# A two-layer graph network: moving the graph product off fp32 and staggering three groups over an unrolled slot schedule

## The chip, the core and the metric

The kernel runs on one core of a Trainium2 chip. A core has five engines that run their own instruction queues in order and meet only through semaphores: TensorE (PE, with its weight loads shown as PEld), VectorE (DVE), ScalarE (ACT), GpSimd (POOL) and SyncE (SP), which here issues every DMA. The metric is the device time of one execution in microseconds (us), lower is better.

## What is computed

`x` has 128 graphs of 128 nodes with 256 features, `adj` is one dense 128 by 128 matrix of weights. Layer 0 is a graph product, a 256 by 256 product, a residual and a layer norm. Layer 1 is three steps of a gated update in which `in_mat` and `out_mat` are both `adj`, then a residual and a layer norm.

```python
x = layernorm(x + (adj @ x) @ W0 + b0)
h = x
for _ in range(3):
    a = adj @ h;  av = concat(a, a)
    z = sigmoid(av @ w3.T + b3 + h @ u3.T + bu3)
    r = sigmoid(av @ w4.T + b4 + h @ u3.T + bu3)
    hv = tanh(av @ w5.T + b5 + (r * h) @ u5.T + bu5)
    h = (1 - z) * h + z * hv
out = layernorm(x + h)
```

Since both halves of `av` are equal, both kernels add the two halves of w3, w4 and w5 once. They also put w3 - w4 in the place of w3, so that z's sum is r's sum, already in PSUM, plus one more product.

## The kernel before

**Tiles.** The 128 graphs go in 32 groups of `G` = 4. A state is kept with features on the partitions: `[128, C=2, 512]`, 512 columns being 4 graphs of 128 nodes. Each gate product is split in three single-pass products, high by high, low by high and high by low (`split_product`, L307): 12 matmuls of 128x512. The high part is a ScalarE copy to fp32r (`copy`, L463), the low part a VectorE subtraction (`low_part`, L577). A gated slot has five of them (u3, w4, w5, w3, u5), 60 matmuls.

**Graph product.** `graph` (L317) is done in plain fp32: the state with nodes on the partitions (`h_nat`) is the stationary operand, `adjt` the moving one, in 8 matmuls of 128x128 columns, each recorded as two. Its result in PSUM (`ps_x`) has features on the partitions already, so that ScalarE and VectorE read its high and low parts (`a_hi`, `a_lo`) straight from PSUM, with no DMA between.

**State to nodes.** For the next graph product the new state must be turned: VectorE transposes blocks of 32x32 (`state_blocks`, L687), SyncE writes them to DRAM (`to_dram`, L214) and reads them back with the four blocks of partitions exchanged (`to_quadrants`, four DMAs, L220), and ScalarE copies them into `h_nat`. The same trip brings a normed first state (`first_blocks`, L629) and a last state (`last_state_blocks`, L638) to the other layout.

**Stages.** Groups go in 16 pairs. A pair has six slots (`SLOTS`): steps 0 to 2 of group a and of group b, in turn. Within slot i the other group's graph product stands between the two output halves of u5. Layer 0 of the next pair is spread over the slots of this one: its graph product (`first_graph`) in slots 1 and 3, its weight product (`first_weights`, L350, 24 matmuls of 128x256) in slots 2 and 4, its sum, statistics and norm on VectorE. GpSimd adds `b0` to x in `x_bias` (L847). `run_pairs` unrolls the first and the last pair and runs the 14 between as a loop on every engine. The state update on VectorE is three operations on each half of 512 columns: L674 (hv - h), L678 (times z), L680 (plus h).

## Time and profile before

| | us |
|---|---|
| median of 3 runs (lowest, highest) | 1674.75 (1674.03, 1675.79) |
| the profiled execution | 1671.51 |
| its span in the trace | 1669.7 |
| TensorE, matmuls at work | 1643.2 |
| VectorE at work | 1364.2 |
| ScalarE at work | 836.8 |
| GpSimd at work | 162.4 |
| moved by DMA in the span | 166.48 MB |

The span is the time from the first to the last record of the profiled execution. Busy times are sums of the durations that the profiler recorded; a matmul's recorded end is modelled and overlaps the next one's start, so the distance between starts is what a matmul costs. An engine's idle time counts only if something on the way to the end waits for it. TensorE's granted clock is full (1.00) over the stretch shown with the rows.

### The profile page before, as it was taken

How to read it: one execution, taken by the hardware profiler on the slowest of the kernel's cores; microseconds unless marked ns; L12 is line 12 of the kernel's file. 1: busy time of each engine (PE TensorE's matmuls, PEld its weight loads, DVE VectorE, ACT ScalarE, POOL GpSimd, SP SyncE). 2: the span in 40 equal slices, each digit the busy share in tenths (PEclk: the TensorE clock that was granted, in tenths of full speed). 3: DMA queues.
4: the chain of work that ended last, by engine and by line, in shares of the span. 5: the costliest groups of instructions: out<-in, count | busy, mean ns of one | idle time of the engine just before them, and what ended most of it. 6: DMA issues, size and time to landing. Idle time of an engine off the chain costs nothing.

```text
span 1669.7 us, 24669 instructions
## 1 busy us (share of the span) xinstructions
PE 1643.2 (98%) x8608; PEld 1410.7 (84%) x8608; DVE 1364.2 (82%) x2217; ACT 836.8 (50%) x1190; POOL 162.4 (10%) x168
## 2 busy tenths in 40 slices
PE   6999999999999999999999999999999999999997
PEld 6888888888888888888888888888888888888885
DVE  5678888888888888888888878888888888888777
ACT  3445454554545454545445454545455455545553
POOL 3001001010100101001010010100101010010000
PEclk8999999999999999999999999999999999999998
DMA  3123242232422333224232332424224232243221
GB/s 112 51 76 126 82 125 83 88 126 96 123 87 83 126 109 105 88 88 136 90 118 83 99 115 88 126 82 125 84 86 126 98 125 86 82 128 110 91 75 63
DMA packets 172021, 166.48 MB, mean 100 GB/s; under 512 B 16352, under 2 KB 147936, under 8 KB 172000
## 3 DMA queue, kind: packets, MB, share of 16 engines
q1 hardware_dynamic: 172000, 166.20, 31.2%
q8 instruction: 13, 0.21, 0.1%
q14 instruction: 8, 0.07, 0.0%
HBM read 84.35 MB, written 81.79 MB: 100 GB/s over the span
## 4 chain that ended last, share of the span: by engine, by line
PE 91%; DVE 4%; SPq 1%; DMA 1%; issue 1%; ACT 1%; DVEq 0%
PE ps_r L307 44%; PE ps_h L307 29%; PE ps_x L317 10%; PE ps_z L350 5%; PE ps_z L317 3%; DVE hv L678 1%; SPq L220 1%; DVE hv L674 1%; DMA h_moved_in<-h_scratch 1%; DVE h_blocks L687 1%; DMA x_in_b<-x 0%; DVE h_t_a L680 0%; ACT hv L499 0%; DVE w_lo L577 0%; ACT h_nat L463 0%
## 5 line engine op out<-in xcount | busy, mean ns | idle before, releaser
L558 ACT ACTIVATE z_sb<-ps_r,bias_z 128x512 f32<-128x512 f32 x192 | 129.9, 686 | 96.9 <-PE ps_r L307 96.7
L499 ACT ACTIVATE hv<-ps_h,bias_h 128x512 f32<-128x512 f32 x192 | 132.3, 689 | 86.2 <-PE ps_h L307 85.9
L674 DVE TENSOR_TENSOR hv<-hv,h_t_a 128x512 f32<-128x512 f32 x96 | 78.3, 815 | 118.9 <-ACT hv L499 118.9
L535 ACT ACTIVATE rh<-ps_r,bias_r 128x512 f32<-128x512 f32 x192 | 126.6, 684 | 91.9 <-PE ps_r L307 90.9
L678 DVE TENSOR_TENSOR hv<-hv,z_sb 128x512 f32<-128x512 f32 x192 | 160.7, 837 | 7.8
L577 DVE TENSOR_TENSOR rh_lo<-rh,rh_hi 128x512 fp32r<-128x512 f32 x192 | 128.4, 689 | 9.4
L463 ACT ACTIVATE rh_hi<-rh 128x512 fp32r<-128x512 f32 x192 | 119.6, 630 | 28.5 <-DVE rh L762 28.5
L317 PEld LDWEIGHTS ps_x<-adjt,h_nat 128*128 128x128 f32 x1024 | 123.4, 191 | 8.7 <-ACT h_nat L463 4.3
L307 PE MATMUL ps_h<-rh_hi,u_hi 128*128 128x512 f32 x384 | 127.1, 412 | 0.0
L317 PE MATMUL ps_x<-adjt,h_nat 128*128 128x128 f32 x1024 | 125.3, 275 | 1.2 <-ACT h_nat L463 1.2
L307 PE MATMUL ps_r<-a_hi_b,w_hi 128*128 128x512 f32 x384 | 121.3, 397 | 0.0
L463 ACT ACTIVATE h_hi_a<-h_t_a 128x1024 fp32r<-128x1024 f32 x48 | 50.7, 1056 | 138.2 <-DVE h_t_a L680 138.1
L307 PE MATMUL ps_r<-a_hi_a,w_hi 128*128 128x512 f32 x384 | 119.3, 392 | 0.0
L307 PE MATMUL ps_r<-a_hi_a,w_lo 128*128 128x512 f32 x384 | 118.9, 391 | 0.0
L307 PE MATMUL ps_h<-rh_hi,u_lo 128*128 128x512 f32 x384 | 118.7, 390 | 0.0
L307 PE MATMUL ps_r<-a_hi_b,w_lo 128*128 128x512 f32 x384 | 118.4, 389 | 0.0
L307 PE MATMUL ps_r<-a_lo_a,w_hi 128*128 128x512 f32 x384 | 118.4, 389 | 0.0
L307 PE MATMUL ps_r<-a_lo_b,w_hi 128*128 128x512 f32 x384 | 118.2, 389 | 0.0
L307 PE MATMUL ps_h<-rh_lo,u_hi 128*128 128x512 f32 x384 | 118.2, 389 | 0.0
L463 ACT ACTIVATE h_hi_b<-h_t_b 128x1024 fp32r<-128x1024 f32 x48 | 50.7, 1056 | 109.1 <-DVE h_t_b L680 109.1
L762 DVE TENSOR_TENSOR rh<-rh,h_t_a 128x512 f32<-128x512 f32 x96 | 64.9, 691 | 46.1 <-ACT rh L535 45.7
L674 DVE TENSOR_TENSOR hv<-hv,h_t_b 128x512 f32<-128x512 f32 x96 | 64.9, 676 | 45.0 <-ACT hv L499 44.5
(141 smaller groups left out, 3749.2 us busy)
## 6 DMA issues: line engine op xcount, KB each, us to landing
h_scratch<-h_blocks SPq DMA_DIRECT2D x128, 256.0 KB, 2.0
h_moved_in<-h_scratch SPq DMA_DIRECT2D x512, 64.0 KB, 2.0
h_scratch<-h_blocks SPq DMA_DIRECT2D x30, 512.0 KB, 2.6
x_in_a<-x SPq DMA_DIRECT2D x16, 512.0 KB, 4.7
x_in_b<-x SPq DMA_DIRECT2D x16, 512.0 KB, 5.7
out<-result_a SPq DMA_DIRECT2D x16, 512.0 KB, 3.0
h_moved_in_a<-h_scratch SPq DMA_DIRECT2D x60, 128.0 KB, 3.5
h_moved_in_b<-h_scratch SPq DMA_DIRECT2D x60, 128.0 KB, 3.0
```

The lines of the kernel that those rows point to most:

```text
L220: sp.dma_start(moved_in[to * Q:(to + 1) * Q].rearrange("q i m e -> q i (m e)"), by_target[to]).then_inc(moved, 16)
L307: mm = pe.matmul(psum[:, o, :], w[:, c, o * P:(o + 1) * P], v[:, c, :], start=start and n == 0 and c == 0, stop=stop and ends, skip_group_ ...
L317: mm = pe.matmul(psum[:, c, b * N:(b + 1) * N], nat[:, b, c * P:(c + 1) * P], adjt[:, :], start=True, stop=True)
L350: mm = pe.matmul(by_node(psum)[:, b, :], v[:, c, cols], w[:, c, :], start=n == 0 and c == 0, stop=n == 2 and c == C - 1, skip_group_check= ...
L463: return act.activation(dst, src, ACT.Copy)
L499: act.activation(hv[:, c, :], ps_h[:, c, :], ACT.Tanh, bias=bias_h[:, c:c + 1]).then_inc(hv_ready, 1)
L535: r = act.activation(rh[:, c, :], ps_r[:, c, :], ACT.Sigmoid, bias=bias_r[:, c:c + 1])
L558: z = act.activation(z_sb[:, c, :], ps_r[:, c, :], ACT.Sigmoid, bias=bias_z[:, c:c + 1])
L577: return dve.tensor_tensor(dst, full, hi.bitcast(F32), ALU.subtract)
L674: dve.tensor_tensor(hv[:, c, :], hv[:, c, :], before[:, c, :], ALU.subtract).then_inc(diff_ready, 1)
L678: dve.tensor_tensor(hv[:, c, :], hv[:, c, :], z_sb[:, c, :], ALU.mult).then_inc(scaled_ready, 1)
L762: dve.tensor_tensor(rh[:, c, :], rh[:, c, :], before[:, c, :], ALU.mult).then_inc(rh_ready, 1)
```

## The change

Everything is rewritten, in one step:

- **The graph product** is split as the gate products are: `adj` is the stationary operand in a high and a low part, the state with nodes on the partitions (`nat_hi`, `nat_lo`) the moving one: 6 matmuls of 128x512. Its result `ps_a` now has nodes on the partitions. It is turned like a state: VectorE transposes it out of PSUM (`graph_blocks`), SyncE writes it to DRAM (`write_a`) and reads it back (`read_a`) into `a_landed`, and `a_hi`, `a_lo` are made from that.
- **Slots.** Step t of group g stands in slot s = 3g + 4t. So three groups are under way, each at another step, and between two steps of one group stand three slots of other work. The slots run from -6 (layer 0 of group 0) to 101. Slots 1, 2, 5, 96, 99 and 100 have no gated step; 96 have one. Within iteration s: the graph product of slot s+1, then the u3 product of slot s, layer 0 of a later group, then the other gates of slot s.
- **Layer 0** is at s mod 3 = 0 (graph product) and 2 (weight product); a group's first state is moved at 1; the last residual and its statistics are at 1. The two norms move from VectorE to ScalarE, with a scale and a shift that GpSimd works out.
- **No loop:** all slots are written out on each engine.
- On VectorE an iteration begins with the state update of slot s-1 (three operations of 1024), then the transposes of the graph result of slot s+1.

```diff
-            def graph(psum, nat, signal):
-
-                for c in range(C):
-                    for b in range(G):
-                        mm = pe.matmul(psum[:, c, b * N:(b + 1) * N], nat[:, b, c * P:(c + 1) * P], adjt[:, :],
-                                       start=True, stop=True)
-                mm.then_inc(signal, 1)
...
+    def slot_of(g, t):
+        return 3 * g + 4 * t
...
+            def graph(s):
+                n = nth[s]
+                pe.wait_ge(nat_hi_ready, n + 1)
+                if n >= 1:
+                    pe.wait_ge(a_blocks_ready, n)
+                for c in range(C):
+                    for k, (w, v) in enumerate(((adj_hi, nat_hi), (adj_lo, nat_hi), (adj_hi, nat_lo))):
+                        if c == 0 and k == 2:
+                            pe.wait_ge(nat_lo_ready, n + 1)
+                        mm = pe.matmul(ps_a[:, c, :], w[:, :], v[:, c, :], start=k == 0, stop=k == 2,
+                                       skip_group_check=True)
+                mm.then_inc(a_done, 1)
...
+            def write_a(s):
+                n, half = nth[s], nth[s] % 2
+                sp.wait_ge(a_blocks_ready, n + 1)
+                if n >= 2:
+                    sp.wait_ge(a_moved[half], (n // 2) * MOVED)
+                to_dram(a_scratch[half], a_blocks[half][:, :, :, :].rearrange("p j c x -> p j (c x)"), a_written[half])
+
+            def read_a(s):
+                n, half = nth[s], nth[s] % 2
+                sp.wait_ge(a_written[half], (n // 2 + 1) * 16)
+                if n >= 2:
+                    sp.wait_ge(a_lo_ready, n - 1)
+                to_quadrants(a_landed[half][:, :, :, :], a_scratch[half], a_moved[half])
...
+            for s in range(BEGIN, END + 5):
+                h0_next = group_at(s, NORM + 1)
+                if h0_next is not None:
+                    write_h0(h0_next)
+                if s + 1 in nth:
+                    write_a(s + 1)
+                if h0_next is not None:
+                    read_h0(h0_next)
+                if s + 1 in nth:
+                    read_a(s + 1)
+                if (g := group_at(s, RESULT + 1)) is not None:
+                    store(g)
+                if (g := group_at(s, GRAPH - 2)) is not None and g >= 2:
+                    load(g)
+                if s - 1 in nth:
+                    move_h(s - 1)
...
+            def first_graph(g):
+                pe.wait_ge(x_loaded[g % 2], (g // 2 + 1) * 16)
+                if g >= 1:
+                    pe.wait_ge(y_added, g)
...
+            def graph_blocks(s):
+                n, half = nth[s], nth[s] % 2
+                dve.wait_ge(a_done, n + 1)
+                if n >= 2:
+                    dve.wait_ge(a_written[half], (n // 2) * 16)
+                for c in range(C):
+                    tr = dve.transpose(a_blocks[half][:, :, c, :].rearrange("p i (b e) -> p i b e", e=Q),
+                                       ps_a[:, c, :].rearrange("p (i b f) -> p i b f", b=G, f=Q))
+                tr.then_inc(a_blocks_ready, 1)
...
+            def graph_low(s):
+                n, half = nth[s], nth[s] % 2
+                dve.wait_ge(a_hi_ready, n + 1)
+                low_part(in_quadrants(a_lo[half]), chunks_first(a_landed[half]),
+                         in_quadrants(a_hi[half])).then_inc(a_lo_ready, 1)
...
+            def update(s):
+                n, (g, t) = nth[s], at(s)
+                state = chunks_first(h_t[g % H_RING])
+                dve.wait_ge(hv_ready, 2 * n + 2)
+                dve.tensor_tensor(in_quadrants(hv), in_quadrants(hv), state, ALU.subtract).then_inc(diff_ready, 1)
+                dve.wait_ge(z_ready, 2 * n + 2)
+                dve.wait_ge(diff_ready, n + 1)
+                dve.tensor_tensor(hv[:, :, :], hv[:, :, :], z_sb[:, :, :], ALU.mult).then_inc(scaled_ready, 1)
+                dve.wait_ge(scaled_ready, n + 1)
+                dve.tensor_tensor(state, in_quadrants(hv), state, ALU.add).then_inc(h_ready, 1)
...
+                if s - 1 in nth:
+                    update(s - 1)
+                if s + 1 in nth:
+                    graph_blocks(s + 1)
+                if s - 1 in nth:
+                    state_blocks(s - 1)
+                if s + 2 in nth:
+                    node_low(s + 2)
+                if s in nth:
+                    reset(s)
+                if s + 1 in nth:
+                    state_low(s + 1)
+                    graph_low(s + 1)
+                if (g := group_at(s, GRAPH)) is not None:
+                    first_graph_low(g)
+                if (g := group_at(s, WEIGHTS)) is not None:
+                    first_sum(g)
+                if (g := group_at(s, NORM)) is not None:
+                    first_blocks(g)
+                if (g := group_at(s, SUM_UP)) is not None:
+                    residual(g)
+
...
+            def add_bias(g):
+                pool.wait_ge(ax_done, g + 1)
```

**VectorE, the middle of the program.** Before, from the second half of one slot's work to the next slot (L674, L678, L680 are the update; L577 of `a_lo` reads `ps_x`; `h0_nat` is layer 0's result):

```order
L680 TENSOR_TENSOR h_t_b<-hv,h_t_b 128x512
L577 TENSOR_TENSOR a_lo_a<-ps_x,a_hi_a 128x1024
L687 STREAM_TRANSPOSE h_blocks<-h_t_b 128x4x4x32
L674 TENSOR_TENSOR hv<-hv,h_t_b 128x512
L678 TENSOR_TENSOR hv<-hv,z_sb 128x512
L680 TENSOR_TENSOR h_t_b<-hv,h_t_b 128x512
L687 STREAM_TRANSPOSE h_blocks<-h_t_b 128x4x4x32
L612 TENSOR_TENSOR h0_nat_b<-ps_z,x_bias_b 128x1024
L762 TENSOR_TENSOR rh<-rh,h_t_a 128x512 x2
L577 TENSOR_TENSOR rh_lo<-rh,rh_hi 128x512 x2
L577 TENSOR_TENSOR h_lo_b<-h_t_b,h_hi_b 128x1024
L587 BN_STATS h0_sums<-h0_nat_b 128x6 x4
```

After, one whole iteration with s mod 3 = 2 without its last row (L584, L587, L589 are the update, L549 the graph result's transposes, L501 with `a_lo` the low part that needs the trip through DRAM, L522 and L506 layer 0):

```order
L584 TENSOR_TENSOR hv<-hv,h_t_d 128x1024
L587 TENSOR_TENSOR hv<-hv,z_sb 128x1024
L589 TENSOR_TENSOR h_t_d<-hv,h_t_d 128x2x4x128
L549 STREAM_TRANSPOSE a_blocks_b<-ps_a 128x4x128 x2
L596 STREAM_TRANSPOSE h_blocks_b<-h_t_d 128x1024
L501 TENSOR_TENSOR nat_lo<-h_landed_a,nat_hi 128x1024
L574 TENSOR_TENSOR rh<-rh,h_t_c 128x512 x2
L501 TENSOR_TENSOR rh_lo<-rh,rh_hi 128x512 x2
L501 TENSOR_TENSOR h_lo<-h_t_a,h_hi 128x1024
L501 TENSOR_TENSOR a_lo_b<-a_landed_b,a_hi_b 128x1024
L522 TENSOR_TENSOR x_in_b<-ps_l,x_in_b 128x1024
L506 BN_STATS h0_sums<-x_in_b 128x6 x4
```

The low part of the graph result stood behind a ScalarE copy from PSUM; now it stands in the same iteration as the transposes, with a write to DRAM, a read and a copy between them, and layer 0's sum and the next update stand behind it in VectorE's queue.

**SyncE, the DMA queue, the middle of the program.** Before, one slot's move of the state (two halves) and the write of a first state:

```order
L220 DMA h_moved_in<-h_scratch_0 32x4x128 x4
L220 DMA h_moved_in<-h_scratch_1 32x4x128 x4
L214 DMA h_scratch_0<-h_blocks 128x512
L214 DMA h_scratch_1<-h_blocks 128x512
L220 DMA h_moved_in<-h_scratch_0 32x4x128 x4
L220 DMA h_moved_in<-h_scratch_1 32x4x128 x4
L214 DMA h0_scratch<-h0_blocks 128x1024
```

After, an iteration with s mod 3 = 1 (`a_` is the graph result, `h_t` from `h0_scratch` the first state):

```order
L188 DMA h0_scratch<-h0_blocks 128x1024
L188 DMA a_scratch_b<-a_blocks_b 128x1024
L193 DMA h_t_d<-h0_scratch 32x4x256 x4
L193 DMA a_landed_b<-a_scratch_b 32x4x256 x4
L239 DMA x_in_b<-x 128x4x256
L188 DMA h_scratch_b<-h_blocks_b 128x1024
L193 DMA h_landed_b<-h_scratch_b 32x4x256 x4
```

Each iteration now has two trips, graph result and state, in place of one, and in every third iteration the first state's write and read stand ahead of the read of the graph result.

**TensorE, the end of one slot and the start of the next.** Before:

```order
L307 MATMUL ps_h<-rh_hi,u5_lo 128x512 x2
L307 MATMUL ps_h<-rh_lo,u5_hi 128x512 x2
L317 MATMUL ps_x<-adjt,h_nat 128x128 x8
L307 MATMUL ps_h<-rh_hi,u5_hi 128x512 x2
L307 MATMUL ps_h<-rh_hi,u5_lo 128x512 x2
L307 MATMUL ps_h<-rh_lo,u5_hi 128x512 x2
L307 MATMUL ps_r<-h_hi_a,u3_hi 128x512 x2
L307 MATMUL ps_r<-h_hi_a,u3_lo 128x512 x2
```

After:

```order
L274 MATMUL ps_h<-rh_lo,u5_hi 128x512 x2
L310 MATMUL ps_a<-nat_hi,adj_hi 128x512
L310 MATMUL ps_a<-nat_hi,adj_lo 128x512
L310 MATMUL ps_a<-nat_lo,adj_hi 128x512
L310 MATMUL ps_a<-nat_hi,adj_hi 128x512
L310 MATMUL ps_a<-nat_hi,adj_lo 128x512
L310 MATMUL ps_a<-nat_lo,adj_hi 128x512
L274 MATMUL ps_r<-h_hi,u3_hi 128x512 x2
L274 MATMUL ps_r<-h_hi,u3_lo 128x512 x2
```

The graph product stands between two slots now, in 6 matmuls of 512 columns in place of 8 of 128 that are recorded twice.

## Rows read from the trace of the kernel before

**Rows 1.** engines of the whole span, page part 1: busy us (share) xinstructions.
```profile
PE 1643.2 (98%) x8608; PEld 1410.7 (84%) x8608; DVE 1364.2 (82%) x2217; ACT 836.8 (50%) x1190; POOL 162.4 (10%) x168
```

**Rows 2.** TensorE: stretch of 50 to 1650 us, and its one wait there.
```profile
50.00:1650.00 1600.00, 1598.77 (x8384) 1372.20 (x8383) 1322.27 (x2136) 814.84 (x1163) 145.26 (x148) 1.00 0.31 100
...
PE ps_x L317 <- ACT h_nat L463: 1.2, 5, 0.3
```

**Rows 3.** timeline of TensorE: start us, us, engine line operation out<-in xcount.
```profile
802.61 1.95 PE L317 MATMUL ps_z<-adjt,x_in_b 128*128 128x128 f32 x16
804.31 0.71 PE L307 MATMUL ps_r<-a_hi_b,w_hi 128*128 128x512 f32 x2
804.86 0.62 PE L307 MATMUL ps_r<-a_hi_b,w_lo 128*128 128x512 f32 x2
...
813.47 0.61 PE L307 MATMUL ps_h<-rh_lo,u_hi 128*128 128x512 f32 x2
...
819.81 0.28 PE L350 MATMUL ps_z<-w_hi,ax_hi 128*128 128x256 f32 x1
...
822.68 0.63 PE L307 MATMUL ps_r<-a_hi_a,w_hi 128*128 128x512 f32 x2
```

**Rows 4.** timeline of VectorE, half a state update (columns as in Rows 3).
```profile
1639.75 0.69 DVE L674 TENSOR_TENSOR hv<-hv,h_t_a 128x512 f32<-128x512 f32 x1 [3.13 <-ACT hv L499]
1640.48 0.69 DVE L678 TENSOR_TENSOR hv<-hv,z_sb 128x512 f32<-128x512 f32 x1
```

**Rows 5.** groups on VectorE by form: shapes xcount; busy us, mean ns; idle before.
```profile
L577 DVE TENSOR_TENSOR h_lo_b<-h_t_b,h_hi_b 128x1024 fp32r<-128x1024 f32 x48 | 58.6, 1221 | 5.5 <-ACT h_hi_b L463 5.5
...
L687 DVE STREAM_TRANSPOSE h_blocks<-h_t_b 128x512 f32<-128x512 f32 x64 | 45.2, 706 | 3.4
...
L587 DVE BATCH_NORM_STATS2 h_sums<-h_nat_a 128x6 f32<-128x256 f32 x64 | 22.4, 412 | 0.0
...
L612 DVE TENSOR_TENSOR h_nat_b<-ps_z,x_bias_b 128x1024 f32<-128x1024 f32 x15 | 18.3, 1218 | 1.2 <-PE ps_z L350 1.2
...
L594 DVE BATCH_NORM_AGGREGATE h_meanvar<-h_sums 128x2 f32<-128x6 f32 x132 | 12.3, 155 | 0.1
```

**Rows 6.** timeline of the DMA issues on SyncE (SPq), one stretch.
```profile
847.29 0.34 SPq L214 DMA_DIRECT2D h_scratch<-h_blocks  x1
849.91 1.73 SPq L220 DMA_DIRECT2D h_moved_in_b<-h_scratch  x4
851.68 0.43 SPq L214 DMA_DIRECT2D last_scratch_a<-last_blocks_a  x1
855.35 1.73 SPq L220 DMA_DIRECT2D last_moved_in_a<-last_scratch_a  x4
...
865.22 1.76 SPq L220 DMA_DIRECT2D last_moved_in_b<-last_scratch_b  x4
```

**Rows 7.** DMA from 865 to 870 us, slices of 0.125 us: busy tenths.
```profile
DMA  0000000004039557988986999987753000000000
```

**Rows 8.** one group on ScalarE by form (columns as in Rows 5).
```profile
L463 ACT ACTIVATE h_hi_b<-h_t_b 128x1024 fp32r<-128x1024 f32 x48 | 50.7, 1056 | 109.1 <-DVE h_t_b L680 109.1
```

**Rows 9.** timeline of GpSimd and VectorE, the same stretch.
```profile
862.41 2.37 POOL L847 TENSOR_TENSOR x_bias_a<-x_in_a,bias_row 128x1024 f32<-128x1024 f32 x1 [25.40 <-DMA x_in_a<-x]
864.74 2.85 POOL L847 TENSOR_TENSOR x_bias_b<-x_in_b,bias_row 128x1024 f32<-128x1024 f32 x1
...
863.95 1.38 DVE L674 TENSOR_TENSOR hv<-hv,h_t_a 128x512 f32<-128x512 f32 x1 [2.60 <-ACT hv L499]
865.45 2.68 DVE L678 TENSOR_TENSOR hv<-hv,z_sb 128x512 f32<-128x512 f32 x1
```

**Rows 10.** timeline of the whole core at its start and its end.
```profile
17.64 1.86 DVE L709 TENSOR_TENSOR w_raw<-w_raw 128x512 f32<-128x512 f32 x3
...
35.59 1.20 PE L307 MATMUL ps_r<-a_hi_a,w_hi 128*128 128x512 f32 x2
...
1665.65 1.28 SPq L291 DMA_DIRECT2D out<-result_b  x2
```

## What the change does to the time

> **What bounds the kernel now.** I read the page's engine totals first. TensorE is at work for 98% of the span, VectorE for 82%, ScalarE 50% [rows 1]. Recorded matmuls overlap, so 98% alone proves little. The next view does: from 50 to 1650 us TensorE works 1598.77 of 1600 us at full granted clock, and its only wait there is for `h_nat`, 1.2 us in five times [rows 2]. So TensorE's own stream sets the time, and a matmul costs the distance between starts. From 804.86 to 813.47 there are 38 of 128x512: 0.2266 us each. An fp32 graph product takes 1.70 us (802.61 to 804.31), and the first pair behind it 0.55 in place of 0.45, so 1.80. Layer 0's weight product takes 2.87 [rows 3]. A pair of groups is 6 slots of 60 x 0.2266 + 1.80 = 15.40, plus 2 x 1.80 and 2 x 2.87: 101.7 us. Sixteen are 1628 of 1669.7; 42 us are start and end.
>
> **TensorE after.** The graph product becomes 6 x 0.2266 = 1.36 in place of 1.80. A slot is 66 x 0.2266 = 14.96, and layer 0 adds 1.80 where s mod 3 is 0 and 2.87 where it is 2. Three slots: 16.76 + 14.96 + 17.83 = 49.55, or 16.52 a slot against 16.95 before. The gain is 0.44 x 96 = 42 us if nothing else binds.
>
> **VectorE after: a loop through DRAM.** Let U be the start of an update. Behind it in the same queue stand, in this order, the graph result's transposes, the state's transposes, `nat_lo`, reset, `h_lo`, `a_lo`, a layer 0 or residual part, and the next update. `a_lo` waits for the trip of what was transposed in this same iteration. So from update to update:
> - update: three dependent operations of 1024. Halves of 0.69 start 0.73 apart [rows 4], a wide one takes 1.22 [rows 5], so 3 x 1.26 = 3.77.
> - transposes of `ps_a`: two of 512, 0.70 and 0.63 more: 1.33. No row shows a transpose out of PSUM. Lower bound 1.33, as from SBUF [rows 5]; upper 2.6, if each cost what a wide one does. The sum and subtraction that read PSUM take 1.22, as those from SBUF do [rows 5], so I take 1.33.
> - write to DRAM: 512 KB, from its issue to the issue of the read that waits for it 2.62 alone (847.29 to 849.91), 3.67 with reads just ahead (851.68 to 855.35) [rows 6].
> - read: four DMAs of 128 KB take 1.76 to issue from 865.22 [rows 6]; DMA engines are busy until 869.0 [rows 7]. I take 3.8.
> - ScalarE's high part 1.06 [rows 8] and 0.1 of semaphores; `a_lo` 1.22 [rows 5].
>
> That is 13.9 us. VectorE's own work between transposes and `a_lo` is 1.2 + 1.2 + 2.7 + 1.2 = 6.3 against 7.6 for the trip, so the trip ends last and VectorE idles about 1.3. Behind `a_lo`:
> - s mod 3 = 0: `ax_lo` and the first state's transposes, 2.3. GpSimd's bias add falls into this iteration's update. In the rows two adds of 2.37 and 2.85 stretched two VectorE operations of 0.69 to 1.38 and 2.68 [rows 9]: 2.7 lost for two, 1.3 for one. 17.5.
> - s mod 3 = 1: residual 1.22, four statistics 1.4, aggregation 0.4: 3.05. The first state's write and read share the DMA engines, so the write is 3.67: 18.0.
> - s mod 3 = 2: sum and statistics, 3.05: 16.95.
>
> Three make 52.45, or **17.48 a slot, above TensorE's 16.52**. A rule bears on the bias add. The Trainium skill (SBUF — State Buffer, section SBUF: two separate sides) says that GpSimd and a VectorE operation with two SBUF inputs share a port pair as an exclusive lock, and whoever comes second waits the whole instruction. By it up to 2.4 would be lost per add, 33 us more in all; the rows show such a conflict, but at 1.3 an add, which I keep. A second: the Trainium skill (DMA: Bandwidth & Descriptors, Anatomy of one DMA) gives about 2.0 us plus bytes over 436 GB/s for a DMA of another issue path. By that estimate a 512 KB write is 3.2, 0.6 above the row; if so, 55 us more.
>
> Everything else is covered. The state's trip (update in iteration s, read back about U + 17) is wanted three slots later. `h_lo` and `nat_lo` are ready before TensorE's 1.36 and 4.08 us into the next slot. Each iteration issues 10 to 16 DMAs at 0.44, at most 7 us. The norms on ScalarE (8 operations of 256 in three slots) fit: it was 50% busy. GpSimd's longer chain of four small operations hides in an iteration.
>
> **Start, holes and end.** These cannot overlap, since the slots beside them are missing. Worked through queue by queue with the same durations:
> - Start. Until the weight sums at 17.64 [rows 10] nothing changes. Then sum and statistics to 20.8, GpSimd to 23.3, norm on ScalarE 24.8, transposes 26.1, first state landed 32.4, `a_lo` of slot 0 at 41.8 (VectorE's weight low parts at 30.7, transposes, trip). TensorE's `first_graph(2)` waits for the sum of group 1, which stands behind that `a_lo`: 43; gates of slot 0 from about 46 (35.59 before, rows 10), end 57.5.
> - Slots 1 and 2 are empty: update 62.3, state to nodes, graph of slot 3, its trip, group 2's sum behind it: gates of slot 3 from 81 to 92. Slot 4 ends at 105.6. Slot 5 is empty: gates of slot 6 wait again, end about 134. The update of slot 6 starts at 136. Four slots have taken 136 us; by TensorE's rate and the old start they would take about 95.
> - Iterations 7 to 95, 89 of them, in steady state: 29 x 52.45 + 34.95 = 1556, to 1692.
> - End. Slots 96, 99 and 100 are empty. From 1692: slot 97's gates end at +24, slot 98's at +37. The last slot then needs update, state to nodes (5.0 + 1.2), graph 1.4, transposes, a trip behind the state's own, high and low part: gates start at +57, end at +68. Update, transposes and trip to +80, residual and statistics, GpSimd, norm and store (3.0) to +89.5.
>
> Span 136 + 1556 + 89.5 = 1781. The profiled execution lies 1.8 over its span and 3.2 under the median, so 1781 + 5 = **1786 us**, 111 slower.
>
> **Rivals.**
> 1. *TensorE bound in the steady state.* If the trip were 3 us shorter a slot (a read that lands sooner, no bias conflict), TensorE's 49.55 would hold: 29 x 49.55 + 32.8 = 1470, time 136 + 1470 + 89.5 + 5 = 1700. For it: VectorE's own work is only some 15.5 a slot. Against it: two trips of rows at their shortest already give 16.95.
> 2. *A dearer loop.* Transposes from PSUM at 2.6 (+1.3 a slot, 116) or the write at 3.67 in every iteration (+0.7 a slot, 62), since traffic rises from 166 MB (the table of the profile) to about 270 MB (512 KB each way, twice in each of 96 slots, and first states, x and out 32 times): 1848 to 1902.
> 3. *Faster.* If the holes cost nothing, because other groups' products and layer 0 fill them, and TensorE bounds all the rest: 32 x 49.55 = 1586 plus the old 42, and 5: 1633. It decides where start, holes and end together lose less than 84 us over TensorE's stream. My sum has 110 (225 for 7 slots of 16.5). Against it: in slots 1, 2 and 5 the queue holds nothing but a graph product that waits for the chain just listed, and `first_graph`, which waits for a sum behind `a_lo`.
> 4. *Equal.* Only a mixture of 1 and 3 gives it.
>
> **How the numbers follow.** The forecast, the loop through DRAM, 0.58 (1750 to 1815 by itself: start and end 15 either way, conflict 0 to 2.4). Rival 1, 0.19. Rival 2, 0.18. Rival 3, 0.04. Rival 4, 0.01. The range leaves out rival 3, equality and the upper part of rival 2: 1695 to 1860. A measurement of this kernel can tell about 0.2%, 3 us, from no change; faster by more 0.04, within 0.01, slower 0.95.
>
> **What would show it.** A steady state of 17.0 to 18.0 us a slot. VectorE waiting for `a_hi` at `a_lo` about 1 us a slot; TensorE waiting at u5 for `rh_lo`, or at the update's followers, about 1 us a slot in the middle and tens of us in the first 136 and last 90. Write to read issue of `a_scratch` 2.6, and 3.7 where s mod 3 = 1. Graph matmuls 0.227 apart. Transposes of `ps_a` about 0.7. Bias add beside a stretched update. It is wrong if TensorE has no waits between 140 and 1690 (rival 1), if `ps_a` transposes take over 1 us or writes 3.7 throughout (rival 2), or if slot 6 ends before 110 us (rival 3).

## The result, and the profile after

| | before | after |
|---|---|---|
| median, us (lowest, highest) | 1674.39 (1671.73, 1675.79) | 1845.02 (1843.4, 1848.24) |
| span of the profiled execution | 1669.7 | 1841.6 |

The changed kernel takes 1.1024 times as long, 95% interval 1.1003 to 1.1044. It is slower, as forecast, by 171 us where 111 were expected. The time is inside the range, but above the 1750 to 1815 us that the prediction gave the loop through DRAM by itself, and 3 us from the lower end of rival 2 (1848 to 1902).

The page's engine totals and the chain of work that ended last answer to [rows 1]. TensorE was at work for 98% of the span; it now has 90%, and the chain runs over VectorE and the DMAs:

```profile
PE 1659.3 (90%) x7616; PEld 1364.3 (74%) x7616; DVE 1431.6 (78%) x1902; ACT 934.9 (51%) x1353; POOL 304.7 (17%) x295
...
DMA 32%; DVE 31%; issue 12%; ACT 11%; PE 7%; SPq 7%; DVEq 0%; POOL 0%; ACTq 0%; POOLq 0%
```

Busy time by stretch of the kernel after (length, then TensorE, its weight loads, VectorE, ScalarE, GpSimd; then granted clock, DMA share, GB/s), which answers to [rows 2]:

```profile
0.00:50.00 50.00, 26.30 (x114) 23.08 (x115) 21.48 (x40) 12.00 (x17) 8.06 (x16) 0.85 0.38 125
50.00:140.00 90.00, 72.08 (x331) 58.62 (x331) 58.11 (x71) 40.01 (x55) 11.27 (x13) 0.93 0.36 117
140.00:1740.00 1600.00, 1503.44 (x6962) 1238.43 (x6961) 1301.47 (x1721) 848.29 (x1229) 277.32 (x255) 0.99 0.49 154
1740.00:1840.00 100.00, 57.54 (x215) 44.15 (x213) 50.51 (x72) 34.59 (x54) 8.02 (x12) 0.80 0.30 98
```

In the middle TensorE idles 97 us of 1600 (1 us before), at a granted clock of 0.99. The waits say for what (engine, what it waits for: us in all, times, longest):

```profile
ACT a_hi_b L384 <- DMA a_landed_b<-a_scratch_b: 178.9, 46, 15.1
ACT a_hi_a L384 <- DMA a_landed_a<-a_scratch_a: 173.9, 48, 6.3
...
DVE a_lo_a L501 <- ACT a_hi_a L384: 137.4, 47, 6.2
DVE a_lo_b L501 <- ACT a_hi_b L384: 133.1, 48, 7.8
...
PE ps_r L274 <- ACT z_sb L460: 98.5, 69, 3.4
...
DVE hv L584 <- ACT hv L464: 50.0, 39, 6.1
```

ScalarE waits for the graph result to come back from DRAM, VectorE waits for ScalarE, and TensorE waits to write `ps_r` again, since ScalarE reads it for `z_sb` only after `a_hi`.

The loop of the prediction can be read from VectorE's timeline of the kernel after, one iteration with s mod 3 = 1, from update to update:

```profile
904.02 1.23 DVE L584 TENSOR_TENSOR hv<-hv,h_t_b 128x1024 f32<-128x1024 f32 x1 [0.75 <-ACT hv L464]
...
907.75 1.31 DVE L549 STREAM_TRANSPOSE a_blocks_b<-ps_a 128x512 f32<-128x512 f32 x2
...
918.44 1.23 DVE L501 TENSOR_TENSOR a_lo_b<-a_landed_b,a_hi_b 128x1024 fp32r<-128x1024 f32 x1 [3.42 <-ACT a_hi_b L384]
919.58 1.22 DVE L538 TENSOR_TENSOR h_nat_d<-h_nat_d,h_landed_a 128x1024 f32<-128x1024 f32 x1
...
922.64 1.19 DVE L584 TENSOR_TENSOR hv<-hv,h_t_a 128x1024 f32<-128x1024 f32 x1
```

The trip inside it, on SyncE and ScalarE, first in this iteration, then in the next (s mod 3 = 2), whose queue holds no first state:

```profile
909.08 0.34 SPq L188 DMA_DIRECT2D a_scratch_b<-a_blocks_b  x1
909.51 2.21 SPq L193 DMA_DIRECT2D h_t_c<-h_scratch  x4
...
912.05 1.73 SPq L193 DMA_DIRECT2D a_landed_b<-a_scratch_b  x4
...
917.35 1.06 ACT L384 ACTIVATE a_hi_b<-a_landed_b 128x1024 fp32r<-128x1024 f32 x1 [4.19 <-DMA a_landed_b<-a_scratch_b]
...
927.67 0.34 SPq L188 DMA_DIRECT2D a_scratch_a<-a_blocks_a  x1
...
930.31 1.73 SPq L193 DMA_DIRECT2D a_landed_a<-a_scratch_a  x4
...
934.65 1.06 ACT L384 ACTIVATE a_hi_a<-a_landed_a 128x1024 fp32r<-128x1024 f32 x1 [2.89 <-DMA a_landed_a<-a_scratch_a]
```

Write to read 2.97 and 2.64 us, read to `a_hi` 5.30 and 4.34. Over the 88 iterations between 140 and 1690 us these distances average 3.05 + 5.92 = 8.97 beside a first state and 2.74 + 4.34 = 7.08 elsewhere.

One table serves the whole study: the distance from update to update by s mod 3, averaged over 57 iterations in the middle of each trace (s from 32 to 88), and where steady state begins (update of slot 6) and ends (update of slot 95). TensorE's own share of three slots is 49.55 by the prediction.

| kernel | median | mod 1 | mod 2 | mod 0 | three | slot 6 | slot 95 |
|---|---|---|---|---|---|---|---|
| prediction | 1786 | 18.0 | 16.95 | 17.5 | 52.45 | 136 | 1692 |
| after | 1845.02 | 19.23 | 17.54 | 17.40 | 54.18 | 143.49 | 1745.13 |
| e1 transposes first | 1696.3 | 15.62 | 17.20 | 16.76 | 49.58 | 141.23 | 1601.11 |
| e2 first state late | 1844.05 | 17.37 | 19.62 | 17.46 | 54.45 | 143.54 | 1746.89 |
| e3 parts early | 1787.93 | 17.49 | 17.67 | 17.41 | 52.58 | 135.20 | 1690.33 |
| e4 no trip | 1674.2 | 15.13 | 17.69 | 16.76 | 49.58 | 124.84 | 1584.44 |
| e5 norms early | 1810.17 | 19.39 | 17.48 | 16.49 | 53.36 | 142.94 | 1713.17 |
| e6 no bias add | 1841.31 | 19.38 | 17.60 | 17.37 | 54.35 | 143.47 | 1745.89 |
| e8 three edits | 1688.84 | 15.22 | 17.60 | 16.76 | 49.58 | 133.79 | 1593.67 |
| e9 holes | 1690.05 | 15.22 | 17.60 | 16.76 | 49.58 | 134.95 | 1595.93 |
| e10 state read last | 1791.21 | 17.59 | 17.50 | 17.33 | 52.42 | 144.82 | 1692.62 |
| e11 quarter state | 1806.3 | 18.02 | 17.52 | 17.37 | 52.90 | 144.74 | 1708.47 |
| e12 = e3 + e5 | 1723.97 | 17.47 | 16.43 | 16.76 | 50.66 | 133.14 | 1631.67 |
| e13 = e3 + e5 + e10 | 1696.29 | 15.68 | 18.02 | 16.04 | 49.74 | 132.20 | 1597.71 |

The kernel before ran beside each batch at 1671.85 (e1 to e4), 1672.52 (e5 to e9) and 1674.14 us (e10 to e13); the ratios below are to it.

### The profile page after: what moved, and what is told of

Same layout as the page of the kernel before. It is cut to its first block, busy times and chain, and to the rows that moved or that the text cites. A ratio compares the mean times of both kernels' runs of the same rounds, so it can differ in the third digit from the quotient of the medians.

```text
span 1841.6 us, 21577 instructions
## 1 busy us (share of the span) xinstructions
PE 1659.3 (90%) x7616; PEld 1364.3 (74%) x7616; DVE 1431.6 (78%) x1902; ACT 934.9 (51%) x1353; POOL 304.7 (17%) x295
## 4 chain that ended last, share of the span: by engine, by line
DMA 32%; DVE 31%; issue 12%; ACT 11%; PE 7%; SPq 7%; DVEq 0%; POOL 0%; ACTq 0%; POOLq 0%
DMA a_landed_a<-a_scratch_a 9%; DMA a_landed_b<-a_scratch_b 8%; DMA a_scratch_a<-a_blocks_a 7%; DMA a_scratch_b<-a_blocks_b 7%; DVE hv L587 6%; SPq L193 6%; DVE hv L584 6%; PE ps_r L274 4%; DVE a_blocks_b L549 3%; DVE a_blocks_a L549 3%; DVE out_sums L506 2%; DVE h_sums L506 2%; PE ps_h L274 2%; ACT hv L464 2%; ACT a_hi_b L384 2%
## 5 line engine op out<-in xcount | busy, mean ns | idle before, releaser
L274 PE MATMUL ps_r<-h_hi,u_hi 128*128 128x512 f32 x384 | 137.8, 442 | 99.1 <-ACT z_sb L460 98.5
L669 POOL TENSOR_TENSOR out_var_eps_sb<-out_meanvar,eps 128x4 f32<-128x4 f32 x32 | 33.4, 1043 | 990.5 <-DVE out_meanvar L512 990.5
L274 PEld LDWEIGHTS ps_r<-h_hi,u_hi 128*128 128x128 f32 x384 | 71.8, 204 | 143.7 <-ACT z_sb L460 132.3
L501 DVE TENSOR_TENSOR a_lo_a<-a_landed_a,a_hi_a 128x1024 fp32r<-128x1024 f32 x48 | 58.8, 1226 | 137.6 <-ACT a_hi_a L384 137.4
L501 DVE TENSOR_TENSOR a_lo_b<-a_landed_b,a_hi_b 128x1024 fp32r<-128x1024 f32 x48 | 58.8, 1226 | 133.1 <-ACT a_hi_b L384 133.1
L384 ACT ACTIVATE a_hi_b<-a_landed_b 128x1024 fp32r<-128x1024 f32 x48 | 50.9, 1060 | 183.7 <-DMA a_landed_b<-a_scratch_b 178.9
L384 ACT ACTIVATE a_hi_a<-a_landed_a 128x1024 fp32r<-128x1024 f32 x48 | 50.9, 1059 | 173.9 <-DMA a_landed_a<-a_scratch_a 173.9
L501 DVE TENSOR_TENSOR rh_lo<-rh,rh_hi 128x512 fp32r<-128x512 f32 x192 | 125.4, 689 | 9.3
L274 PE MATMUL ps_r<-h_lo,u_hi 128*128 128x512 f32 x384 | 127.9, 416 | 1.0 <-DVE h_lo L501 1.0
L274 PE MATMUL ps_r<-h_hi,u_lo 128*128 128x512 f32 x384 | 128.4, 418 | 0.0
L587 DVE TENSOR_TENSOR hv<-hv,z_sb 128x1024 f32<-128x1024 f32 x96 | 117.7, 1226 | 10.0
```

Source lines behind the costliest of these rows:

```text
L274: mm = pe.matmul(psum[:, o, :], w[:, c, o * P:(o + 1) * P], v[:, c, :], start=start and n == 0 and c == 0, stop=stop and n == 2 and c == C ...
L384: return act.activation(dst, src, ACT.Copy)
L501: return dve.tensor_tensor(dst, full, hi.bitcast(F32), ALU.subtract)
L587: dve.tensor_tensor(hv[:, :, :], hv[:, :, :], z_sb[:, :, :], ALU.mult).then_inc(scaled_ready, 1)
L669: pool.tensor_tensor(var_eps[:, :], meanvar[:, :, 1], eps[:, :], ALU.add).then_inc(eps_added, 1)
```

## Experiments

**e1: is it the order on VectorE?** The transposes of the graph result go ahead of the update.

```diff
+                if s + 1 in nth:
+                    graph_blocks(s + 1)
                 if s - 1 in nth:
                     update(s - 1)
-                if s + 1 in nth:
-                    graph_blocks(s + 1)
```

> One edit to the changed kernel: on VectorE the graph result's transposes stand ahead of the last slot's update instead of behind it. Theory A (a loop in VectorE's queue bounds the steady state: update, transposes, write, read, a_lo, sum, next update): the update's 3.8 us leave the loop and lie beside the trip, the loop falls under TensorE's 16.5 us a slot, and 89 slots at 16.5 to 17.0 in place of 18.0 give 1710 to 1755 us. Theory B (the DMA engines' load makes the trips long, whatever the order): under 20 us gained, above 1825. Theory C (TensorE's u3 waiting for z_sb from ScalarE is the bound): z_sb stands behind a_hi in ScalarE's queue, so it gains as in A where a_hi comes earlier, but the waits of u3 for z_sb stay at their 98 us.

1696.3 us, ratio 1.0149 (1.0132 to 1.0166). Three slots take 49.58: the steady state is TensorE's, which is never idle (busy time of 150 to 1550 us in e1, then in the kernel after):

```profile
150.00:1550.00 1400.00, 1400.00 (x6709) 1181.25 (x6708) 1271.68 (x1662) 826.35 (x1181) 215.04 (x251) 1.00 0.53 170
```

```profile
150.00:1550.00 1400.00, 1318.23 (x6145) 1088.28 (x6144) 1141.13 (x1517) 744.52 (x1077) 252.43 (x230) 0.99 0.49 155
```

The 3.73 us of the update leave the loop and hide beside the trip. One swap of two steps is worth 149 us, somewhat more than theory A gave (its range ended at 1710): 142 us lie between the updates of slots 6 and 95, the rest at start and end. The time is near rival 1's 1700, which priced a steady state at TensorE's rate.

**e4: what is the trip worth?** `write_a` and `read_a` are left out, and `a_hi` and `a_lo` are made from `a_blocks`; the four blocks of partitions are then not exchanged, so a part of the computation is missing. The semaphore waits follow the tiles, and `a_lo` changes as `a_hi` does; the diff shows the main lines.

```diff
-                if s + 1 in nth:
-                    write_a(s + 1)
...
-                if s + 1 in nth:
-                    read_a(s + 1)
...
-                copy(in_quadrants(a_hi[half]), chunks_first(a_landed[half])).then_inc(a_hi_ready, 1)
+                copy(in_quadrants(a_hi[half]), chunks_first(a_blocks[half])).then_inc(a_hi_ready, 1)
```

> The graph result's write to DRAM and read back are left out: a_hi and a_lo are made from the transposed blocks themselves, so that the blocks of partitions are not exchanged. Nothing else is changed. Theory A: without 7 us of trip the loop is VectorE's own work, under TensorE's 16.5 us: 89 slots at 16.5 to 16.9, and about 30 us less in start, holes and end, where four trips stood in line: 1670 to 1710. Theory C (ScalarE and TensorE's wait for z_sb by itself): above 1780.

1674.2 us, ratio 1.0014 (1.0004 to 1.0023). With the trip gone and the order as it is, the steady state is TensorE's again (49.58). Even then the kernel is no faster than the one before: start and end stay long.

**e2: the first state's share.** Its write and read go behind the graph result's trip on SyncE.

```diff
-                if h0_next is not None:
-                    write_h0(h0_next)
                 if s + 1 in nth:
                     write_a(s + 1)
-                if h0_next is not None:
-                    read_h0(h0_next)
-                if s + 1 in nth:
                     read_a(s + 1)
+                if h0_next is not None:
+                    write_h0(h0_next)
+                    read_h0(h0_next)
```

> One edit to the changed kernel: on SyncE the first state's write and read stand behind the write and read of the graph result instead of around them. Theory A: where s mod 3 = 1 the read of the graph result is issued at once after its write and lands 4.35 us later, as in the other slots, in place of 5.3 and about 0.3 us of issue: that iteration falls from 19.3 to 17.7, 31 times, about 45 us: 1795 to 1810. Theory B (total load): no change, 1835 to 1850, because the same bytes move.

1844.05 us, ratio 1.1025 (1.1002 to 1.1047): nothing gained. The iterations with s mod 3 = 1 fall from 19.23 to 17.37 and the next ones rise from 17.54 to 19.62. The state's own trip now stands behind the first state's, and SyncE's queue carries it into the next iteration (timelines of SyncE and VectorE in e2; the transposes of `ps_a` start at 927.50):

```profile
919.54 1.73 SPq L193 DMA_DIRECT2D h_t_c<-h_scratch  x4
...
927.84 1.74 SPq L193 DMA_DIRECT2D h_landed_b<-h_scratch_b  x4
929.68 0.44 SPq L188 DMA_DIRECT2D a_scratch_a<-a_blocks_a  x1
933.63 1.73 SPq L193 DMA_DIRECT2D a_landed_a<-a_scratch_a  x4
...
933.54 1.23 DVE L499 TENSOR_TENSOR nat_lo<-h_landed_b,nat_hi 128x1024 fp32r<-128x1024 f32 x1 [3.61 <-ACT nat_hi L382]
...
939.22 1.22 DVE L499 TENSOR_TENSOR a_lo_a<-a_landed_a,a_hi_a 128x1024 fp32r<-128x1024 f32 x1 [0.34 <-ACT a_hi_a L382]
```

The graph result's write is issued behind the state's four reads, and its bytes move with theirs. In these iterations it is issued 2.22 us after the transposes start in place of 1.34, and its read follows after 3.62 us in place of 2.80. That is 1.70 of the 2.08 us. VectorE stops at `nat_lo` too, but it still waits for `a_hi` at `a_lo`, so that stop is not what ends last. So e2 gives theory B's number without showing its reason: it moves the cost to another iteration, and only e10 can tell the theories apart.

**e10: only the reads change places.** The first state's write stays, its four reads go behind the graph result's four.

```diff
-                if h0_next is not None:
-                    read_h0(h0_next)
                 if s + 1 in nth:
                     read_a(s + 1)
+                if h0_next is not None:
+                    read_h0(h0_next)
```

> SyncE issues the four reads of the first state behind the four of the graph result instead of ahead of them; the first state's write stays where it was. Theory A (the iterations with s mod 3 = 1 are longer because the graph result's read is issued and served behind the first state's four reads: 5.30 us instead of 4.35): those iterations fall by about 1 us, and nothing comes late for it, since the first state is issued only some 3 us later: 32 x 1.0, 1808 to 1818 us. Rival B (the two writes side by side cost it, 2.97 instead of 2.64, and the reads only look like it): 1835 to 1845. Rival C (as when the whole first state's trip stood behind: the next iteration pays): 1840 to 1850.

1791.21 us, ratio 1.0713 (1.0697 to 1.0728): 54 us less, more than theory A gave. The iterations with s mod 3 = 1 fall by 1.64, and no other rises. The trip beside a first state averages 2.73 + 4.49 = 7.22 us in place of 8.97: both the write and the read of the graph result had been late. In SyncE's timeline of e10 both sets of reads follow each other:

```profile
934.61 0.34 SPq L188 DMA_DIRECT2D a_scratch_a<-a_blocks_a  x1
937.63 1.74 SPq L193 DMA_DIRECT2D a_landed_a<-a_scratch_a  x4
939.48 1.79 SPq L193 DMA_DIRECT2D h_t_d<-h_scratch  x4
```

**e11: bytes or place?** The order of the change is kept, but from the sixth group on only a quarter of the first state is moved.

```diff
-                to_dram(h0_scratch, h0_blocks[:, :, :], h0_written)
+                j = BLOCKS if g < H_RING else 1
+                to_dram(h0_scratch[0:j * Q], h0_blocks[0:j * Q, :, :], h0_written)
...
-                to_quadrants(h_t[g % H_RING][:, :, :, :], h0_scratch, h0_moved)
+                j = BLOCKS if g < H_RING else 1
+                to_quadrants(h_t[g % H_RING][:, 0:j, :, :], h0_scratch[0:j * Q], h0_moved)
```

> From the sixth group on, only a quarter of the first state is written and read (128 KB in place of 512 KB each way, still one and four DMAs), so that three quarters of these states are those of an earlier group. It prices the bytes of the first state's trip by themselves. The prediction put the whole trip at 1.05 us a group: by that about 1815 us. If it is the 1.9 us by which the iterations with s mod 3 = 1 stand above those with 2 (19.3 against 17.4): 27 x 1.9, about 1793 us. If the count of DMAs in the queue and not their bytes is what costs: 1835 to 1845.

1806.3 us, ratio 1.0796 (1.078 to 1.0812). That is between the two prices (1815 and 1793). Three quarters of the bytes are worth 1.21 us an iteration, less than their place in the queue (1.64). So most of the price is in the bytes that are served ahead of the graph result's. What is left is not an even price for the place: over the 27 iterations with a quarter state the trip averages 2.80 + 4.80 = 7.60 us against 7.22 in e10, but read to `a_hi` is 4.27 in the 14 with odd s, as without any first state, and 5.36 in the 13 with even s. The buffers `a` and `b` change with the same parity; why one of them pays stays open.

**e5: ScalarE's queue.** The norms go ahead of `graph_high`.

```diff
-                if s + 1 in nth:
-                    graph_high(s + 1)
                 if (g := group_at(s, NORM)) is not None:
                     first_norm(g)
                 if (g := group_at(s, RESULT)) is not None:
                     result_norm(g)
+                if s + 1 in nth:
+                    graph_high(s + 1)
```

> Only the order on ScalarE changes: the four-part norm of layer 0 or of the result (2.07 us in the trace of the changed kernel) stands ahead of the high part of the graph result instead of behind it. Theory A (two loops of nearly one length in the iterations with s mod 3 = 0: VectorE waits 0.75 us for hv because ScalarE's queue carries a_hi, norm, z and hv in line): the norm now runs while the trip is still on its way, the 0.75 us wait and a part of what was hidden behind it go, 0.7 to 1.0 us in 32 iterations, 1815 to 1825 us. Rival (the trip alone, ScalarE only looks like it): no change, 1840 to 1850 us. A third way is a loss: if the norm is not ready before the trip lands (it waits for GpSimd's scale), a_hi stands behind it and the time grows to 1860 or more.

1810.17 us, ratio 1.0809 (1.0782 to 1.0836): theory A, with some more than it gave. In the kernel after, s mod 3 = 0 looks thus on ScalarE, with the update that waits for it on VectorE:

```profile
898.66 1.06 ACT L384 ACTIVATE a_hi_a<-a_landed_a 128x1024 fp32r<-128x1024 f32 x1 [2.61 <-DMA a_landed_a<-a_scratch_a]
899.63 2.07 ACT L396 ACTIVATE h_nat_c<-x_in_b,h_shift,h_rstd_sb 128x256 f32<-128x256 f32 x4
...
901.60 1.24 ACT L460 ACTIVATE z_sb<-ps_r,bias_z 128x512 f32<-128x512 f32 x2
...
902.74 1.25 ACT L464 ACTIVATE hv<-ps_h,bias_h 128x512 f32<-128x512 f32 x2
```

The norm stands between what waits for the trip and what the next update waits for. Moved ahead, it runs while the trip is out, and these iterations fall by 0.91 us, to 16.49.

**e3: VectorE's queue.** Layer 0's parts and the residual go ahead of `graph_low`.

```diff
                     state_low(s + 1)
-                    graph_low(s + 1)
                 if (g := group_at(s, GRAPH)) is not None:
                     first_graph_low(g)
                 if (g := group_at(s, WEIGHTS)) is not None:
                     first_sum(g)
-                if (g := group_at(s, NORM)) is not None:
-                    first_blocks(g)
                 if (g := group_at(s, SUM_UP)) is not None:
                     residual(g)
+                if s + 1 in nth:
+                    graph_low(s + 1)
+                if (g := group_at(s, NORM)) is not None:
+                    first_blocks(g)
```

> One edit to the changed kernel: on VectorE layer 0's low part and sum and the residual with their statistics stand ahead of a_lo, in the idle time before it, instead of behind it. Theory A with VectorE alone in the loop: 3.05 us leave two of three iterations as far as idle time takes them (4.6 and 2.1), 30 times: 1845 - 30 x (3.05 + 2.1) = 1690. Theory A with ScalarE's queue beside it (a_hi, norm of 2.07, z, hv end at the same time as VectorE where s mod 3 is 0 and 2): only s mod 3 = 1 gains, until hv is there, 1.9 us, 30 times: about 1785.

1787.93 us, ratio 1.0689 (1.0664 to 1.0715). Some 3 us leave VectorE's loop in two iterations of three, but the iterations fall by 0.5 us on average (54.18 to 52.58 for three): the other branch takes over. Timelines of ScalarE and VectorE in e3, s mod 3 = 0 and then 1:

```profile
921.12 1.06 ACT L384 ACTIVATE a_hi_b<-a_landed_b 128x1024 fp32r<-128x1024 f32 x1 [2.25 <-DMA a_landed_b<-a_scratch_b]
922.08 2.06 ACT L396 ACTIVATE h_nat_d<-x_in_a,h_shift,h_rstd_sb 128x256 f32<-128x256 f32 x4
924.05 1.24 ACT L460 ACTIVATE z_sb<-ps_r,bias_z 128x512 f32<-128x512 f32 x2
925.19 1.25 ACT L464 ACTIVATE hv<-ps_h,bias_h 128x512 f32<-128x512 f32 x2
...
926.47 1.23 DVE L584 TENSOR_TENSOR hv<-hv,h_t_c 128x1024 f32<-128x1024 f32 x1 [1.05 <-ACT hv L464]
...
940.60 1.06 ACT L384 ACTIVATE a_hi_a<-a_landed_a 128x1024 fp32r<-128x1024 f32 x1 [4.99 <-DMA a_landed_a<-a_scratch_a]
...
944.00 1.22 DVE L584 TENSOR_TENSOR hv<-hv,h_t_b 128x1024 f32<-128x1024 f32 x1 [1.09 <-ACT hv L464]
```

From `a_hi` to the next update it is 5.35 with a norm between and 3.40 without. So the ring has two ways home, VectorE's (`a_lo` and what is behind it) and ScalarE's (norm, `z_sb`, `hv`).

**e12 and e13: both ways home, then the reads too.** e12 has the edits of e3 and e5, e13 that of e10 as well. The update stays ahead of the transposes in both.

> The order under study is kept (update ahead of the graph result's transposes), but layer 0's parts and the residual stand ahead of a_lo on VectorE, and the norms ahead of a_hi on ScalarE. Alone the first took 1788 us and the second 1810. If the two savings add: 1753. Theory A (a ring: update, transposes, trip, a_hi, then either VectorE's queue or ScalarE's z and hv lead to the next update; each edit alone leaves the other branch): with both shorter the ring is 11.9 + 3.4 = 15.3 us where s mod 3 is 0 or 2, under TensorE's 16.5, and only the iterations with the first state's trip (about 17.5) stay above TensorE's 15.2: about 1 to 2.3 us in 32 iterations over the 1689 us of the kernel with all three edits: 1705 to 1740.

1723.97 us, ratio 1.0297 (1.0281 to 1.0312). The two save 57 and 35 us alone and 121 together, so they don't add: each alone leaves the other way home. That is theory A's ring, in its range. What is left above TensorE's share is the iterations with s mod 3 = 1, 17.47.

> As the kernel before it, with the first state's reads behind the graph result's as well. The update still stands ahead of the graph result's transposes. By theory A every iteration is now shorter than or level with TensorE's share, and it comes to 1688 to 1705 us: then the order named in the change costs time only together with what else stands in the ring. If the order costs by itself, 1715 us or more.

1696.29 us, ratio 1.0144 (1.0128 to 1.0159), the same as e1. TensorE is busy for all but 1.7 us of 1400 (e13, 150 to 1550 us):

```profile
150.00:1550.00 1400.00, 1398.32 (x6694) 1177.28 (x6693) 1256.30 (x1662) 814.99 (x1182) 300.56 (x251) 1.00 0.53 169
```

So the order that the change names costs 149 us beside the parts, the norms and the reads where they stand, and little once these three are out of the ring. It is not shown to be nothing: e8 below, with the swap in place of e10's edit, is 7.5 us faster (1688.84), 5.6 of them between the updates of slots 6 and 95. That e13 and e1 agree to 0.01 us is chance: e13 reaches slot 6 9.0 us sooner and loses that again after it.

**e6: GpSimd's bias add.** Cut to 8 of 256 columns; b0 is left out of the others.

```diff
-                pool.tensor_tensor(x_in[g % 2][:, :, :], x_in[g % 2][:, :, :],
-                                   bias_row[:, :].unsqueeze(1).to_broadcast([P, G, D]), ALU.add).then_inc(x_biased, 1)
+                pool.tensor_tensor(x_in[g % 2][:, :, 0:8], x_in[g % 2][:, :, 0:8],
+                                   bias_row[:, 0:8].unsqueeze(1).to_broadcast([P, G, 8]), ALU.add).then_inc(x_biased, 1)
```

> GpSimd's bias add of layer 0 is cut from 256 to 8 columns a graph, so b0 is left out of the other 248 features. It prices the conflict between GpSimd and VectorE by itself. The prediction put it at 1.3 us for each of 32 adds: by that 1800 to 1808 us. By the trace of the changed kernel a low part beside the add takes 1.50 instead of 1.18 and the loop's stretched part is only partly on the path: 0 to 0.3 us an add, 1835 to 1845 us.

1841.31 us, ratio 1.1016 (1.0991 to 1.104): not to be told from the change itself. In the kernel after, the add runs here, beside transposes and a low part (GpSimd and VectorE):

```profile
890.69 2.41 POOL L661 TENSOR_TENSOR x_in_a<-x_in_a,bias_row 128x1024 f32<-128x1024 f32 x1
...
892.67 1.51 DVE L501 TENSOR_TENSOR nat_lo<-h_landed_b,nat_hi 128x1024 fp32r<-128x1024 f32 x1
```

The low part takes 1.51 in place of 1.18, and VectorE waits for the trip soon after, which swallows the third of a microsecond. The loss is small because the add is nearly over: it ends at 893.10, 0.43 us after the low part starts. Where it has more left, the low part loses more (same engines, later in the kernel after):

```profile
1597.75 2.40 POOL L661 TENSOR_TENSOR x_in_b<-x_in_b,bias_row 128x1024 f32<-128x1024 f32 x1 [1.09 <-PE ps_l L286]
...
1598.60 2.64 DVE L501 TENSOR_TENSOR nat_lo<-h_landed_a,nat_hi 128x1024 fp32r<-128x1024 f32 x1
```

Here 1.55 us of the add are left and 1.46 are lost. In each of the 27 adds that a low part `nat_lo` runs into, it loses what is left of the add less about 0.1 us.

**e8 and e9: what the best of it gives.** e8 has the edits of e1, e3 and e5. e9 adds that, in iterations beside an empty slot, `node_high` (on ScalarE) and `node_low` (on VectorE, shown) stand ahead of the work of the slot before:

```diff
+                if s + 2 in nth and s not in nth:
+                    node_low(s + 2)
                 if s - 1 in nth:
                     update(s - 1)
...
-                if s + 2 in nth:
+                if s + 2 in nth and s in nth:
                     node_low(s + 2)
```

> Three edits at once: the graph result's transposes ahead of the update, layer 0's parts ahead of the low part that needs the trip, the norm ahead of the high part. With the first of them alone the kernel took 1696.3 us, and its steady state was TensorE's 49.55 us for three slots. If TensorE bounds the steady state, the other two can only shorten the waits at the start and the end, where layer 0 of the second group stood behind the low part of the first slot: 5 to 15 us less, 1681 to 1692 us. If the steady state still had VectorE's loop in some iterations, more goes, to 1670 to 1680. The other way, layer 0's sum ahead of a_lo delays a_lo where it stood on the path: 1696 to 1705.

1688.84 us, ratio 1.0091 (1.0076 to 1.0105). Steady state as in e1; slot 6 is reached 7.4 us sooner than in e1, since layer 0 of the second group no longer stands behind `a_lo` of slot 0 (e3, with that move alone, has 8.3 us of it against the kernel after).

> As the kernel with the three edits, and in the iterations beside a slot that has no gated step (slots 1, 2, 5, 96, 99, 100) the turned state's high and low part stand ahead of the work of the last slot. It prices one order in the holes: if that order is what makes the holes long, 1665 to 1680 us; if the holes are the dependent chain itself (update, state to nodes, graph product, trip, gates), it changes nothing against the kernel with three edits, within 3 us.

1690.05 us, ratio 1.0106 (1.009 to 1.0122), within 3 us of e8. In e8 TensorE waited 4.55 us at slot 3's graph product for `nat_lo`; that goes, and the wait turns up at slot 4's, 8.93 us (TensorE in e9), which needs the update of slot 0 and its trip whatever stands beside them:

```profile
72.47 0.79 PE L310 MATMUL ps_a<-nat_hi,adj_hi 128*128 128x512 f32 x1 [8.93 <-ACT nat_hi L384]
```

## Why the prediction was right, and where its sum was off

**The mechanism holds.** The loop through DRAM in VectorE's queue sets the steady state (e1 takes the update out of it, e4 the trip, and each gives TensorE's rate). The sum was 60.6 us short in the span: 7.5 at the start, 45.6 in the 89 iterations, 7.0 at the end (96.5 in place of 89.5). By its own signs the steady state, 18.06 us a slot, is just above the 17.0 to 18.0 that it named. The time is that of rival 2's cheaper half, but not by its mechanism: the transposes take 1.31 and not 2.6, and the write 2.74 and not 3.67 in the iterations without a first state. What held the measurement in the range was the room left for rival 2, not the sum.

**Terms that measured as taken.** Update: operations start 1.33 and 1.26 us apart (904.02, 905.35, 906.61 in the trace), 3.73 against 3.77. The transposes of `ps_a` 1.31 against 1.33; from PSUM they cost what they do from SBUF, so the first half of rival 2 falls. High part to low part 1.09 against 1.16. Graph matmuls 0.227 apart, TensorE's three slots 49.58 against 49.55.

**The read was undersized.** "I take 3.8" was put together from issue time and the end of DMA activity [rows 6, 7]; read to `a_hi` is 4.34. With a write of 2.74 for 2.62 the plain trip is 7.08, not 6.42. That is the size of the 0.59 by which s mod 3 = 2 exceeds 16.95.

**The first state was undersized and its mechanism incomplete.** The prediction priced the shared DMA engines at 1.05, on the write alone. Measured, the trip beside a first state is 1.89 us longer than the others, and 1.6 of that is the read. e10 removes 1.64 us by queue order alone. It is the largest error: 1.23 us in each such iteration.

**The bias add's 1.3 us did not happen.** The step "GpSimd's bias add falls into this iteration's update" failed: GpSimd first works out a scale and shift, and the add begins after the update (890.69 against 886.58). It meets one operation with two SBUF inputs, costs 0.33 us there and is covered (e6). The price of 1.3 an add was an average of two unlike cases. In [rows 9] the first add had 0.83 us left and cost 0.69, the second 2.14 left and cost 1.99; here 0.43 and 0.33. So what an add costs follows from when it starts, and the prediction should have timed it. The Trainium skill (SBUF — State Buffer, SBUF: two separate sides) has an exclusive lock: whoever starts first keeps the ports for the whole instruction. The traces agree with it, at 1.55 us left and 1.46 lost as at 0.43 and 0.33.

**ScalarE was waved through.** "The norms on ScalarE (8 operations of 256 in three slots) fit: it was 50% busy" looked at its load, not at its order. A norm of four operations of 256 columns takes 2.07 us and stood behind the wait for the trip; VectorE then waits 0.75 us for `hv`. That s mod 3 = 0 measured 17.40 against 17.5 is luck: the 0.75 and the 0.66 of the longer trip stand in for the bias add's 1.3. Rival mechanisms of this kind, a second way home of the same ring, were not in the list, and e3 shows what that costs a forecast: by VectorE's queue alone 1690 us, in fact 1788.

**Where TensorE waits.** Forecast at u5 for `rh_lo` or at the update's followers; in fact at the next slot's u3, for `z_sb` to have read `ps_r` (98.5 us in 69 waits). VectorE's wait at `a_lo` was put at 1 us a slot and is 2.8 (270.5 in 95).

**Write length.** The Trainium skill (DMA: Bandwidth & Descriptors, Anatomy of one DMA) gave an estimate of 3.2 us for a write of 512 KB by another issue path; 59 writes of SyncE without a first state beside them measured 2.74, nearer the row's 2.62.

**Start and end.** `a_lo` of slot 0 came at 44.11 in place of 41.8, the update of slot 0 4.2 us late (it starts at 62.75; in the prediction it ends at 62.3, so starts at 58.5), that of slot 6 7.5 late. The granted clock is 0.85 in the first 50 us and 0.80 in the last 100, where TensorE works 26.3 and 57.5 us; the sum took every matmul at full clock. How much of the 14.5 us is the clock was not separated.

**Why no version wins.** In e8 TensorE's rate is reached, and start and end still take 133.8 + 93.4 = 227.2 us for seven slots that TensorE would stream in 115.7 (7 x 49.58 / 3). That loss of 111.5 is the prediction's 110. Without the trip (e4) it is still 97, and the time only equals the kernel before. So rival 3's condition, less than 84 us lost, was never met. The kernel before loses 42 us at its start and end by the prediction's sum. The split graph product saves another 42 us on TensorE, and the longer start and end, with three empty slots each, eat them.

## What to carry to other kernels

Where in-order queues close a ring (update, transposes, DRAM trip, high part, next update), sum the ring once along each engine on which it can come home, and expect an edit to one way home to show only the distance to the next. Whatever does not need the trip belongs ahead of the instruction that waits for it: here one swap, or two such moves and the order of the reads, were worth 149 us. Before staggering work to gain a few per cent of rate, price the empty slots at both ends; start and end lost 111 us where they had lost 42, against a gain of 42.

## What the runs showed of the hardware

- Eight reads of 128 KB issued one behind another on one queue: the consumer of the second four starts 5.92 us after their first issue, where with four alone it starts after 4.34. Issued first, with four others behind them, it is 4.49. The first in line pays 0.15.
- With the reads ahead cut to 32 KB each, the four behind take 4.27 us in 14 iterations and 5.36 in the 13 between them: bytes explain most of the price, and the rest is uneven, for a reason that no run here shows.
- A VectorE operation with two SBUF inputs that starts during a GpSimd add from SBUF is longer by what is left of the add, less some 0.1 us (1.55 us left: 2.64 in place of 1.18; 0.43 left: 1.51). Transposes, with one input, beside the same adds keep their 1.31 and 1.20, and a low part that reads PSUM (`ax_lo`, beside the add of 24.52) its 1.23.
- ScalarE takes 2.07 us for four operations of 256 columns and 1.06 for one of 1024 columns, so each small operation costs about 0.52 in a row.
- VectorE transposes blocks of 32x32 from PSUM as fast as from SBUF: 0.69 us for 512 columns against 0.71 from SBUF in the kernel before, 1.31 for two in a row.
